# Masked attention stages: the penalties' matmul ahead of the maxima, scores accumulated on it

## The chip, the cores and the metric

One core of a Trainium2 chip runs the whole program. The time is device microseconds of one execution; the median of several runs stands for a kernel. Engines: PE multiplies matrices (PEld loads its stationary operand), ACT exponentiates and copies, DVE reduces and adds, POOL does small vector work, SP issues DMAs. PE writes into PSUM, which has eight banks of 128 x 512 float32.

## The reference, cut to what matters

Four layers of cross and self attention over x (8 x 512 x 256) follow one another; written as six attention stages s, each is

```
q, k, v = heads of x and of its keys        # 16 heads of 16
scores = q @ k^T * 16 ** -0.5                # 512 x 512 for each head
scores = where(mask, -inf, scores)           # stages 0 and 2 (two masks), stage 3 is causal
x = x + softmax(scores) @ v @ Wo             # then an MLP behind stages 0, 2 and 4
```

The last stage has 64 channels a head and is written as a loop of its own ("tail"). Only stages 0 and 2, the masked ones, are touched here; with 8 batches each they are 16 units of attention.

## The kernel before, in words

A softmax needs a maximum for each row. The kernel computes the scores twice: once roughly in bf16 with the queries along the partitions, for DVE to find the maxima (`max_scores`, L678, into the banks psS), and once in float32 with the keys along the partitions (`exp_scores`, L696, into the four banks psT, with the maximum already subtracted through an extra row of Q and K), for ACT to exponentiate (L991). In the masked stages two of the four heads of a step (j = 0, 1) get their mask as a penalty of -2^100, which a matmul of the identity with a bf16 tile of penalties adds in PSUM (L702); the other two (j = 2, 3) are limited after the exponential by DVE (`limit`, L1180). So a masked step exponentiates the pair 2, 3 first and the pair 0, 1 second.

The loop goes over bodies. A body handles three batches at once: the end of the one before (`prev`: output projection, in stages 0, 2 and 4 the MLP), the attention of the current one (`cur`), and the preparation and part of the maxima of the next (`nxt`). It has 16 steps i, for 4 groups of heads times 4 tiles of keys (kt). In each step PE does, in the order of the program, which is the order in which it executes:

- the maxima listed as `before` for this step (two 32-row matmuls, one for each bank of psS; each waits until DVE has read that bank),
- `exp_scores(i)`: it waits for both exponentials of step i - 1, which read the same four banks; then the scores in float32 (32 rows each, four side by side in the array, eight recorded matmuls), then the penalties (two full 128 x 128 bf16 matmuls),
- fills (transposes L645, projections L650 and L657, maxima as rows L762; one shared bank, `small`),
- the maxima listed as `beside`, the matmuls of the probabilities with V (`outputs(i - 1)`, L721, which wait for the exponentials and for DVE's limit), more fills, the maxima listed as `after`.

In which step which maxima and fills stand is written out by hand (`maxima_plan`, `NXT_USES`, `CUR_USES` and the like). In bodies with an MLP inside (14 of the 16 masked ones) one pair of maxima stands `before` in steps 1 to 8 and 13 to 15, a pair `beside` in steps 13 to 15, and step 12 has one beside and one after; the MLP (L779, L788) stands between steps 9 and 10 and uses psT too. The two other masked bodies have one before and one or two further pairs in each step.

Of the kernel before, what the change touches and what calls it, by code (L numbers as in the profile page):

```python
# [6 lines left out]
P = 128  # L7
B = 8
S = 512
D = 256  # L10
C = D // P
T = S // P
# [27 lines left out]
MASKED = (0, 2)  # L40
CAUSAL = 3
# [241 lines left out]
def positive(n):  # L283

    return not isinstance(n, int) or n > 0


def build(nc, x, ctx, ctxT, maskB, maskBT, maskS, maskST, vecs, wa, wm1, wm2, w5, eye, tri, triT, out):
    with ExitStack() as stack:
        def sb(name, shape, dt=F32):  # L290
            return stack.enter_context(nc.sbuf_tensor(name, shape, dt))
# [4 lines left out]
        def semaphore(name):  # L296
            return stack.enter_context(nc.semaphore(name))

        sem = {n: semaphore(n) for n in PER[0]}
# [33 lines left out]
        def count(name, u, k):  # L333

            return u.b * PER[u.s][name] + (AHEAD.get(name, 0) + B * sum(PER[i][name] for i in range(u.s)) + k)
# [72 lines left out]
        pens = sb("pens_sb", [P, 3, T * S], BF16)  # L408
# [12 lines left out]
        identb = sb("identb", [P, P], BF16)  # L421
        onesb = sb("onesb", [P, P], BF16)
        onesf = sb("onesf", [P, DL])
        trib = sb("trib", [P, 2, P], BF16)
# [11 lines left out]
        pensE = [pens[:, 2, :], out5[:, 1, 6 * S:8 * S].bitcast(BF16)]  # L436
# [34 lines left out]
        def masking(tiles, u):  # L471

            return tiles[u.parity if u.s == 0 else 0]

        def rows_of(j):
            return slice(32 * j, 32 * (j + 1))
# [5 lines left out]
        psT = [psT_all[:, i, :] for i in range(4)]  # L482
# [159 lines left out]
        def _(pe):  # L642
# [18 lines left out]
            def max_scores(place, u, i, k, ahead):  # L661

                g, qt = divmod(i, T)
                c, a, q = g // 2, g % 2, u.parity
                n = (qt + 1) * P if u.s == CAUSAL else S
                if qt == 0 and k == 0 and a == 0:

                    if ahead:
                        wait_taken(pe, place, "nxt", place.last("nxt", f"k{c}"))
                    else:  # L670
                        pe.wait_ge(small_read, place.start() + 1)
                    pe.wait_ge(sem["q_low"], count("q_low", u, c + 1))

                for e in range(2):
                    j = 2 * (1 - k) + e
                    if positive(r := count(f"s_read{e}", u, 2 * i + k)):
                        pe.wait_ge(sem[f"s_read{e}"], r)
                    nc.tensor.matmul(psS[e][:, 0:n], Qb[rows_of(j), q, a, c, qt * P:(qt + 1) * P], Kb[rows_of(j), q, c, 0:n],  # L678
                                     start=True, stop=True).then_inc(sem[f"s_full{e}"], 1)

            def exp_scores(place, u, i):

                g, kt = divmod(i, T)
                c, a, q = g // 2, g % 2, u.parity
                q0 = kt * P if u.s == CAUSAL else 0
                if kt == 0:

                    pe.wait_ge(small_read, place.fills("cur", f"m{g}") + 2 if g else place.start() + 1)
                if u.s == 0 and i == 0:
                    pe.wait_ge(sem["pens"], count("pens", u, 2))  # L690

                if positive(k := count("exp_done", u, 2 * i)):
                    pe.wait_ge(sem["exp_done"], k)
                for j in (2, 3, 0, 1) if u.s in MASKED else range(4):
                    plain = u.s != CAUSAL and not (u.s in MASKED and j < 2)
                    last = nc.tensor.matmul(psT[j][:, q0:S], Kf[rows_of(j), q, a, c, kt * P:(kt + 1) * P], Qf[rows_of(j), q, a, c, q0:S],  # L696
                                            start=True, stop=plain)
                    if plain and j % 2:
                        last.then_inc(sem["st_full"], 1)
                for j in range(2 if u.s in MASKED else 4 if u.s == CAUSAL else 0):  # L700
                    if u.s in MASKED:
                        last = nc.tensor.matmul(psT[j], identb[:], masking(pensE, u)[:, kt * S:(kt + 1) * S], start=False, stop=True)  # L702
                    else:
                        last = nc.tensor.matmul(psT[j][:, q0:q0 + P], identb[:], trib[:, 1, :], start=False, stop=True)
                    if j % 2:
                        last.then_inc(sem["st_full"], 1)

            def outputs(place, u, i):

                g, kt = divmod(i, T)  # L710
                q0 = kt * P if u.s == CAUSAL else 0
                if i in (2, 3):
                    wait_taken(pe, place, "cur", f"v{i}")
                pe.wait_ge(sem["exp_done"], count("exp_done", u, 2 * i + 2))
                if u.s in MASKED:
                    pe.wait_ge(sem["limited"], count("limited", u, i + 1))

                if kt == 0 and positive(k := count("o_out", u, g)):
                    pe.wait_ge(sem["o_out"], k)
                for j in range(4):  # L720
                    last = nc.tensor.matmul(psO[32 * j:32 * j + 32, q0:S], V[:, u.parity, kt, head(g, j), :],  # L721
                                            probs[:, i % 2, j, q0:S], start=kt == 0, stop=kt == T - 1)
                last.then_inc(sem["pv_done"], 1)
# [71 lines left out]
            def mlp(place, u, cur, nxt):  # L795

                def maximum_next(n):
                    if nxt is not None:
                        max_scores(place, nxt, n // 2, n % 2, True)

                if cur is not None:
                    pe.wait_ge(sem["exp_done"], count("exp_done", cur, 2 * (MLP_AFTER + 1)))
                for m in range(FC):
                    hidden(place, u, m)
                    maximum_next(m)
                    if cur is None and m >= FC - T - 1:
                        tail_max_scores(m - (FC - T - 1))
                if cur is not None:
                    outputs(place, cur, MLP_AFTER)
                for t in range(T):  # L810
                    for part in range(2):
                        from_hidden(place, u, t, part)
                        maximum_next(FC + 2 * t + part)

            def body(place, prev, cur, nxt):
                units = (cur, nxt)

                def maxima(pairs):
                    for ahead, n in pairs:
                        max_scores(place, units[ahead], n // 2, n % 2, ahead)  # L820

                for i, (before, beside, after) in enumerate(place.body.maxima()):
                    late = place.body.at(2 * i + 1)
                    long = any(use in ("q0", "q1", "k0", "k1", "w") for _, use in late)
                    after_mlp = place.body.mlp and i == MLP_AFTER + 1
                    maxima(before)
                    if cur is None and nxt is None and i in TAIL_TURNS:
                        for name in TAIL_TURNS[i]:
                            tail_fill(name)
                    if cur is not None:  # L830
                        if after_mlp:
                            pe.wait_ge(sem["z_read"], count("z_read", prev, 1))
                        exp_scores(place, cur, i)
                    for owner, use in place.body.at(2 * i):
                        fill(place, owner, use, prev, cur, nxt)
                    if not long:
                        maxima(beside)
                    of = prev if i == 0 else None if after_mlp else cur
                    limited = of is not None and of.s in MASKED and not (place.body.at(2 * i) and late)
                    if of is not None and not limited:  # L840
                        outputs(place, of, (i - 1) % STEPS)
                    if long:
                        maxima(beside)
                    for owner, use in late:
                        fill(place, owner, use, prev, cur, nxt)
                    if limited:
                        outputs(place, of, (i - 1) % STEPS)
                    maxima(after)
                    if place.body.mlp and i == MLP_AFTER:
                        mlp(place, prev, cur, nxt)  # L850
# [112 lines left out]
            for at in range(T * PAIRS):  # L963
                n, kt = divmod(at, T)
# [633 lines left out]
```

## Time and profile before

| | |
|---|---|
| median of 3 runs | 5038.94 us (5037.19 to 5039.55) |
| the profiled execution | 5035.45 us, span 5033.6 us |
| PE busy | 4666.1 us (93%), 24484 matmuls |
| DVE busy | 3036.8 us (60%) |
| ACT busy | 2308.4 us (46%) |
| POOL busy | 1068.9 us (21%) |
| mean granted clock of PE | 0.976 |

A busy share is a mean over stages. Masked bodies take some 107 to 112 us each; the two masked stages lie at 70 to 931 us and 1544 to 2399 us of the span. In a timeline a row is a run of the same instruction of one line; matmuls overlap and their ends are modelled, so the start of the next row tells more than the end of one.

### The profile page before, as it was taken

The numbers are of one execution on the slowest core, as the hardware profiler recorded it, in microseconds if no ns is written. First come the engines' busy times: TensorE is split into PE (matmuls) and PEld (weight loads), VectorE is DVE, ScalarE is ACT, GpSimd is POOL, SyncE is SP. The second block draws the span as 40 slices with busy tenths as digits, with TensorE's granted clock in tenths as the row PEclk, the third lists the DMA queues.
The fourth block names the chain that finished last, engine by engine and source line by source line (L and its number), as shares of the span: only waits on it lengthen the run. The fifth ranks groups of instructions, "written<-read, shape, count | busy, mean of one in ns | idle before, by whom it ended". The sixth has DMA issues, their size and how long they took to land.

```text
span 5033.6 us, 66240 instructions
## 1 busy us (share of the span) xinstructions
PE 4666.1 (93%) x24484; PEld 1880.0 (37%) x24484; DVE 3036.8 (60%) x7970; ACT 2308.4 (46%) x3011; POOL 1068.9 (21%) x991
## 2 busy tenths in 40 slices
PE   6999999989998999999988889999989999999999
PEld 2333333433332333343444433333333333333333
DVE  6777776556767777665565565555534455545554
ACT  4454554456664444434445454444443333333332
POOL 0111211111111211111111111211113333333333
PEclk9999999999999999999999999999999999999999
DMA  1111111121121111001211121111120000000000
GB/s 60 35 51 52 48 41 44 35 87 56 58 66 51 37 37 33 30 31 42 73 61 56 57 71 42 52 37 35 39 77 21 13 1 13 13 13 13 1 13 9
DMA packets 164465, 201.67 MB, mean 40 GB/s; under 512 B 36273, under 2 KB 119601, under 8 KB 162866
## 3 DMA queue, kind: packets, MB, share of 16 engines
q1 hardware_dynamic: 141106, 176.34, 10.5%
q0 software_dynamic: 23040, 21.10, 1.7%
q8 instruction: 197, 3.23, 0.3%
q14 instruction: 122, 1.00, 0.1%
HBM read 128.86 MB, written 68.42 MB: 39 GB/s over the span
## 4 chain that ended last, share of the span: by engine, by line
PE 61%; issue 19%; DVE 14%; ACT 4%; POOL 1%; DMA 1%; DVEq 0%; SPq 0%; POOLq 0%; ACTq 0%
PE psO L721 8%; PE small L650 8%; PE psT L696 6%; PE small L657 5%; PE psT L926 5%; PE psS L678 4%; PE psT L779 3%; DVE nmb L1171 3%; PE psT L650 2%; PE psT L886 2%; PE psO L941 2%; PE psT L896 2%; PE psT L941 2%; PE psT L702 2%; DVE xn L1148 2%
## 5 line engine op out<-in xcount | busy, mean ns | idle before, releaser
L991 ACT ACTIVATE probs<-psT 128x1024 f32<-128x1024 f32 (+3 forms) x1280 | 1159.7, 960 | 1211.2 <-PE psT L696 1042.0
L1171 DVE TENSOR_REDUCE nmb<-psS 128x1 bf16<-128x512 f32 x1024 | 649.8, 685 | 293.4 <-PE psS L678 292.8
L1168 DVE CUSTOM_DVE_ANT_0 out<-psS,pens_sb 128x512 f32<-128x512 f32 x1024 | 665.4, 685 | 250.4 <-issue 248.7
L696 PE MATMUL psT<-low 32*128 32x512 f32 (+3 forms) x5120 | 755.0, 608 | 29.4 <-ACT probs L991 26.5
L721 PE MATMUL psO<-probs,V 128*32 128x512 f32 (+3 forms) x5120 | 670.5, 597 | 20.6 <-DVE probs L1180 19.0
L678 PE MATMUL psS<-out 32*128 32x512 bf16 (+3 forms) x2560 | 595.6, 380 | 97.1 <-DVE nmb L1168 46.4
L1354 DVE TENSOR_REDUCE parts<-psS 128x2 bf16<-128x1024 f32 x256 | 314.9, 1230 | 531.4 <-PE psS L913 531.4
L1097 ACT ACTIVATE probs<-psT 128x1024 f32<-128x1024 f32 x256 | 262.0, 1023 | 524.9 <-PE psT L929 524.9
L678 PEld LDWEIGHTS psS<-out 32*128 32x128 bf16 x2560 | 148.6, 91 | 796.9 <-issue 444.0
L779 PE MATMUL psT<-out,W 128*128 128x512 f32 x768 | 382.9, 620 | 0.4
L1021 ACT ACTIVATE low<-small,vec 128x256 f32<-128x256 f32 (+1 forms) x464 | 261.9, 617 | 232.8 <-PE small L650 232.7
L1499 POOL TENSOR_TENSOR oN<-oN,probs 128x1024 f32<-128x1024 f32 x128 | 300.6, 2349 | 316.1 <-ACT probs L1097 315.8
L1435 POOL TENSOR_TENSOR var<-mhalf 128x4 f32<-128x4 f32 x80 | 16.9, 211 | 1583.6 <-ACT low L1021 1583.6
L1180 DVE TENSOR_TENSOR probs<-probs,parts 128x1024 f32<-128x1024 f32 x256 | 321.5, 1256 | 50.0 <-ACT probs L991 49.6
L1168 DVE CUSTOM_DVE_ANT_0 out<-psS,tri_row 128x384 f32<-128x384 f32 (+3 forms) x512 | 230.8, 486 | 152.8 <-issue 152.5
L1447 POOL DMA_DIRECT2D oN<-o_mid x160 | 100.2, 631 | 984.1 <-DMA o_mid<-out 870.7
L696 PEld LDWEIGHTS psT<-low 32*128 32x128 f32 x5120 | 253.4, 190 | 120.6 <-issue 80.9
L926 PE MATMUL psT<-V 64*128 64x512 f32 x1024 | 289.0, 641 | 2.2 <-ACT parts L1087 1.0
L650 PE MATMUL small<-hT,Wqkv 128*128 128x256 f32 (+1 forms) x656 | 241.4, 491 | 25.9 <-DVE low L1204 17.2
L1041 ACT ACTIVATE gel<-psT,vec 128x512 f32<-128x512 f32 x192 | 131.9, 687 | 287.1 <-PE psT L779 287.1
L1499 POOL TENSOR_TENSOR oN<-probs 128x1024 f32<-128x1024 f32 x64 | 150.5, 2351 | 412.4 <-ACT probs L1097 412.4
L1204 DVE TENSOR_TENSOR low<-low,small 128x512 f32<-128x512 f32 x160 | 109.6, 685 | 176.0 <-PE small L762 176.0
(178 smaller groups left out, 5942.4 us busy)
## 6 DMA issues: line engine op xcount, KB each, us to landing
o_mid<-out SPq DMA_DIRECT2D x160, 256.0 KB, 2.0
oN<-o_mid POOLq DMA_DIRECT2D x160, 128.0 KB, 3.5
oN<-r_mid SPq DMA_DIRECT2D x80, 256.0 KB
x_mid<-xe SPq DMA_DIRECT2D x40, 512.0 KB, 2.9
xw<-x_mid SPq DMA_DIRECT2D x36, 512.0 KB, 4.1
xe<-x_mid SPq DMA_DIRECT2D x36, 512.0 KB, 5.0
cT<-ctxT SPq DMA_DIRECT2D x20, 512.0 KB, 5.5
W<-wm SPq DMA_DIRECT2D x6, 1024.0 KB, 8.5
```

Of the source, the lines that this page charges most:

```text
L650: last = nc.tensor.matmul(dst[:, tokens], w[:, c, cols], src[:, c, tokens], start=c == 0, stop=c == C - 1)
L678: nc.tensor.matmul(psS[e][:, 0:n], Qb[rows_of(j), q, a, c, qt * P:(qt + 1) * P], Kb[rows_of(j), q, c, 0:n], start=True, stop=True).then_in ...
L696: last = nc.tensor.matmul(psT[j][:, q0:S], Kf[rows_of(j), q, a, c, kt * P:(kt + 1) * P], Qf[rows_of(j), q, a, c, q0:S], start=True, stop=p ...
L721: last = nc.tensor.matmul(psO[32 * j:32 * j + 32, q0:S], V[:, u.parity, kt, head(g, j), :], probs[:, i % 2, j, q0:S], start=kt == 0, stop= ...
L779: last = nc.tensor.matmul(psT[m % 2], W1[:, c, m * P:(m + 1) * P], hM[:, c, :], start=c == 0, stop=c == C - 1)
L926: nc.tensor.matmul(psT[j], K5[n % 3][rows, kt * P:(kt + 1) * P], Q5[n % 3][rows, :], start=True, stop=False)
L991: nc.scalar.activation(probs[:, i % 2, two, q0:S], psT_all[:, two, q0:S], ACT.Exp, scale=float(DH) ** -0.5)\
L1168: nc.vector.tensor_tensor_reduce(junk[:, e, 0:n], psS[e][:, 0:n], penalty, 1.0, -3.0e38, ALU.add, ALU.max, at).then_inc(sem[f"s_read{e}"], 1)
L1171: nc.vector.tensor_reduce(at, psS[e][:, 0:n], AX, ALU.max).then_inc(sem[f"s_read{e}"], 1)
L1180: nc.vector.tensor_tensor(two, two, both, ALU.min).then_inc(sem["limited"], 1)
L1354: nc.vector.tensor_reduce(nmb[n % 2][:, qt, 0:P:DL], psS_both[:], AX, ALU.max, negate=True).then_inc(tail_s_read, 1)
L1499: nc.gpsimd.tensor_tensor(pacc[n % 2], before, P5[kt], ALU.add).then_inc(tail_summed, 1)
```

## The change

The penalties of j = 0, 1 go ahead of everything in a masked step: a new function `penalties` waits for the exponentials of the step before (and, in the first one, for the penalties' tile), then opens the two banks with the identity matmuls (`start=True, stop=False`). Then come the maxima `before`, then the scores, which for j = 0, 1 accumulate on what the bank holds (`start=False`) and close it. The wait for the exponentials thus stands ahead of the maxima in the masked stages; in the others nothing changes. Behind the MLP the wait for its last read of psT moves ahead with the penalties. Number and sizes of all matmuls stay, and the second signal to ACT comes from the scores of j = 1.

```diff
+            def penalties(u, i):
+
+                if positive(k := count("exp_done", u, 2 * i)):
+                    pe.wait_ge(sem["exp_done"], k)
+                if u.s == 0 and i == 0:
+                    pe.wait_ge(sem["pens"], count("pens", u, 2))
+                for j in range(2):
+                    nc.tensor.matmul(psT[j], identb[:], masking(pensE, u)[:, i % T * S:(i % T + 1) * S], start=True, stop=False)
+
             def exp_scores(place, u, i):
...
-                if u.s == 0 and i == 0:
-                    pe.wait_ge(sem["pens"], count("pens", u, 2))
-
-                if positive(k := count("exp_done", u, 2 * i)):
+                if u.s not in MASKED and positive(k := count("exp_done", u, 2 * i)):
                     pe.wait_ge(sem["exp_done"], k)
                 for j in (2, 3, 0, 1) if u.s in MASKED else range(4):
-                    plain = u.s != CAUSAL and not (u.s in MASKED and j < 2)
+                    plain = u.s != CAUSAL
                     last = nc.tensor.matmul(psT[j][:, q0:S], Kf[rows_of(j), q, a, c, kt * P:(kt + 1) * P], Qf[rows_of(j), q, a, c, q0:S],
-                                            start=True, stop=plain)
+                                            start=not (u.s in MASKED and j < 2), stop=plain)
                     if plain and j % 2:
                         last.then_inc(sem["st_full"], 1)
-                for j in range(2 if u.s in MASKED else 4 if u.s == CAUSAL else 0):
-                    if u.s in MASKED:
-                        last = nc.tensor.matmul(psT[j], identb[:], masking(pensE, u)[:, kt * S:(kt + 1) * S], start=False, stop=True)
-                    else:
-                        last = nc.tensor.matmul(psT[j][:, q0:q0 + P], identb[:], trib[:, 1, :], start=False, stop=True)
+                for j in range(4 if u.s == CAUSAL else 0):
+                    last = nc.tensor.matmul(psT[j][:, q0:q0 + P], identb[:], trib[:, 1, :], start=False, stop=True)
                     if j % 2:
                         last.then_inc(sem["st_full"], 1)
...
+                    if cur is not None and cur.s in MASKED:
+                        if after_mlp:
+                            pe.wait_ge(sem["z_read"], count("z_read", prev, 1))
+                        penalties(cur, i)
                     maxima(before)
...
                     if cur is not None:
-                        if after_mlp:
+                        if after_mlp and cur.s not in MASKED:
                             pe.wait_ge(sem["z_read"], count("z_read", prev, 1))
                         exp_scores(place, cur, i)
```

## Rows read from the trace of the kernel before

**Rows 1.** Page, part 5: busy us, mean ns, idle us before, what ended it.

```profile
L991 ACT ACTIVATE probs<-psT 128x1024 f32<-128x1024 f32 (+3 forms) x1280 | 1159.7, 960 | 1211.2 <-PE psT L696 1042.0
```

**Rows 2.** Busy time by stretch: two neighbouring bodies, then both masked stages.

```profile
core 0: us, PE busy (x) PEld busy (x) DVE busy (x) ACT busy (x) POOL busy (x), PEclk, DMA share, GB/s
387.00:498.30 111.30, 105.99 (x540) 43.74 (x540) 78.77 (x265) 55.46 (x63) 20.20 (x23) 0.95 0.14 44
498.30:605.50 107.20, 101.78 (x544) 42.37 (x540) 78.94 (x263) 55.43 (x63) 20.07 (x23) 1.00 0.15 46
...
69.90:930.70 860.80, 804.58 (x4164) 326.93 (x4166) 623.87 (x2010) 429.26 (x496) 145.58 (x167) 0.97 0.14 42
...
1543.90:2399.00 855.10, 795.65 (x4130) 322.07 (x4130) 600.21 (x2019) 386.43 (x462) 138.59 (x162) 0.98 0.12 39
```

**Rows 3.** Timeline of PE, steps 7 to the MLP of one body: start us, us.

```profile
420.27 1.23 PE L696 MATMUL psT<-low 32*128 32x512 f32 x8
...
423.40 0.39 PE L678 MATMUL psS<-out 32*128 32x512 bf16 x2
423.63 1.14 PE L696 MATMUL psT<-low 32*128 32x512 f32 x8
424.70 0.61 PE L702 MATMUL psT<-out,identb 128*128 128x512 bf16 x2
425.14 1.88 PE L650 MATMUL small<-cT,Wqkv 128*128 128x512 f32 x4
...
427.95 1.14 PE L696 MATMUL psT<-low 32*128 32x512 f32 x8
...
431.49 0.59 PE L779 MATMUL psT<-out,W 128*128 128x512 f32 x1
```

**Rows 4.** Timeline of ACT, the same stretch.

```profile
421.55 1.94 ACT L991 ACTIVATE probs<-psT 128x1024 f32<-128x1024 f32 x2 [0.41 <-PE psT L696]
...
429.36 1.96 ACT L991 ACTIVATE probs<-psT 128x1024 f32<-128x1024 f32 x2
```

**Rows 5.** Timeline of PE, step 15 of a body and step 0 of the next.

```profile
602.11 1.23 PE L696 MATMUL psT<-low 32*128 32x512 f32 x8
603.27 0.60 PE L702 MATMUL psT<-pens_sb,identb 128*128 128x512 bf16 x2
603.81 0.64 PE L678 MATMUL psS<-out 32*128 32x512 bf16 x2
...
605.47 1.14 PE L696 MATMUL psT<-low 32*128 32x512 f32 x8
...
606.99 0.39 PE L762 MATMUL small<-identb,nmb 128*128 128x128 bf16 x4
```

**Rows 6.** Timeline of PE, step 14: the second maxima and the fill behind.

```profile
599.47 0.63 PE L678 MATMUL psS<-out 32*128 32x512 bf16 x2
600.03 1.13 PE L657 MATMUL small<-Wqkv,cT 128*128 128x256 f32 x4
```

**Rows 7.** Timeline of DVE, the same step: it reads the maxima's scores.

```profile
598.35 0.69 DVE L1168 CUSTOM_DVE_ANT_0 out<-psS,pens_sb 128x512 f32<-128x512 f32 x1
...
598.97 0.68 DVE L1168 CUSTOM_DVE_ANT_0 out<-psS,pens_sb 128x512 f32<-128x512 f32 x1
...
599.90 0.69 DVE L1168 CUSTOM_DVE_ANT_0 out<-psS,pens_sb 128x512 f32<-128x512 f32 x1 [0.24 <-issue]
```

**Rows 8.** Timeline of PE: idle time in brackets, and who ended it (steps 2, 3, 5, 10).

```profile
397.13 1.07 PE L721 MATMUL psO<-probs,V 128*32 128x512 f32 x8 [0.64 <-DVE probs L1180]
...
401.54 0.66 PE L645 MATMUL small<-ident,xn 128*128 128x128 f32 x4 [1.48 <-DVE xn L1148]
...
412.33 1.97 PE L657 MATMUL small<-Wo,oN 128*128 128x256 f32 x8 [0.25 <-ACT low L1021]
...
909.01 0.38 PE L762 MATMUL small<-identb,nmb 128*128 128x128 bf16 x4 [0.67 <-DVE xe L1243]
```

**Rows 9.** Busy time by stretch, columns as in rows 2: around a fall of the clock.

```profile
399.29:402.70 3.41, 1.43 (x10) 0.53 (x6) 3.41 (x7) 2.68 (x4) 1.40 (x2) 1.00 0.13 41
402.70:406.10 3.40, 3.33 (x18) 1.37 (x22) 2.29 (x6) 0.63 (x2) 0.00 (x0) 0.50 0.43 127
```

## The prediction, made before the change was run

> **What bounds the kernel now.** I read the page first, its costliest groups: ACT, the one engine that exponentiates, idles 1211.2 us before its exponentials, 1042.0 of it for PE's scores [rows 1]. In a masked body PE is busy 101.78 of 107.20 us [rows 2]. So ACT waits for PE in the mean, and removing PE time would pay. But the change removes no instruction; it moves the penalties' 512 matmuls (two a step, 16 steps, 16 masked batches, by the code). What counts is which wait ends last at each place. So I went on to the stretches of one masked body (107.20 and 111.30 us, two neighbours [rows 2]), then to the order of time on PE, ACT and DVE in it. I call the maxima ahead of the scores M, the scores S, the penalties P, output matmuls O, fills F, the second maxima of a step M2; numbers of steps are those of the loop over i.
>
> **The loop through ACT.** In steps 7 to 8, S starts at 420.27, the exponentials run from 421.55 to 423.49, and the next S starts at 423.63 [rows 3, 4]. So from S to the first exponential 1.28 us, both exponentials 1.94, and 0.14 from their end to the next S: 3.36 us, and step 8 is one such period after step 7: PE had come to M at 423.40 [rows 3], M ran in the wait's shadow, and S waited. The same 3.36 stands between steps 15 and 0: S 602.11, S 605.47 [rows 5]. Elsewhere PE's own work is longer than the loop, or DVE is the limit.
>
> **Part 1: P and its wait ahead of M and S.** P costs 0.44 us before a fill (424.70 to 425.14 [rows 3]). Before a 32-row matmul it costs 0.54 (603.27 to 603.81 [rows 5]), since PE drains when the tiling of its array changes; I take 0.54 for P ahead of M. Before, P lay behind S and beside the exponentials; it was outside the loop. After, the order is: exponentials end, P, S, exponentials. The loop becomes 3.36 + 0.54 = 3.90 us. P waits for both exponentials at its start, and behind it in PE's order are M, S and all that follows; M no longer covers the wait, and DVE, which reads M, gets it later. ACT gains nothing from the second pair being ready earlier: its second exponential follows the first at once already (both in one 1.94 stretch [rows 4]).
>
> **Part 2: what that costs, step by step** (bodies with the MLP of the previous batch inside; 14 of the 16 masked batches, 7 in each masked stage).
> - Step 7 to 8: P of step 7 would start where M and S did, 420.27; P of step 8 at 420.27 + 3.90 = 424.17, less 0.1, because step 7's P stands behind a full-array fill and needs no drain: 424.07. Then P 0.54 and M with S 1.16 (602.11 to 603.27 [rows 5]): the fill starts at 425.77, not 425.14. **+0.63**, with no idle time of PE named behind it up to 431.49 [rows 3].
> - Step 9: S moves 0.54 later. Its exponentials end at 431.32 [rows 4], and the MLP's first matmul, which takes the same banks, starts at 431.49 [rows 3]. They began at 429.36, 1.41 after S at 427.95, where 1.28 would do, so 0.13 of the 0.54 is taken up by ACT's own work before them: **+0.4**.
> - Step 14: M2 must wait until DVE has read M. M is read at 598.35 and 598.97, M2 is issued at 599.47 behind P, read at 599.90 [rows 6, 7]. M itself stood at 599.47 - 0.54 - 1.16 - 0.02 = 597.75. After, it comes 0.54 later, at 598.29, its reads start at 598.72 (0.43 after M, as 599.47 to 599.90) and end at 599.96; M2's second half may issue only some 0.14 after that, and what is behind it 0.31 later: 600.41 for the fill that now starts at 600.03. **+0.38**. P behind S no longer fills the time in which DVE reads M.
> - Step 15 to 0: the loop gives 602.11 + 3.90 = 606.01 for P of step 0, then P 0.54 and S without M 1.07 (423.63 to 424.70 [rows 3]): fill at 607.62, now at 606.99 [rows 5]. **+0.63**.
> - Steps 6 and 12 (and 7 in the second masked stage): P between O and M, then a fill, has one drain more than S, P, fill: +0.1 each, **+0.2 to 0.3**. Steps 4 and 11: behind a full-array fill one drain goes and one comes: 0.
> - Steps 1 to 3: the loop is again too long for steps 1 and 2 (0.25 to 0.55 us late). But PE waits 0.64 there for DVE's limits, then 1.48 for the normalised tokens [rows 8]. These waits cover it: 0. With that cover gone it would be +0.8.
> - Step 5: the fill behind P waits 0.25 for ACT's copies in one stage and longer in the other: 0; uncovered +0.3. Step 10: the fill behind P waits 0.67 for DVE's residual sum, and only M's 0.3 and a drain are added ahead of it: 0 [rows 8]. Step 13: M waits for DVE's reads, P slips into that wait, but DVE's order decides when M2 goes: 0, at best -0.44.
> The sum for a body is 0.63 + 0.4 + 0.38 + 0.63 + 0.25 = 2.29 us; times 14 it is 32.1. The two masked bodies without an MLP are bound by DVE's maxima for half their steps: I put 0.5 each, between -3 (P in all waits of M) and +5 (0.3 for each step): **+33 us in all**. The profiled execution took 5035.45 us around a span of 5033.6; so 5068. The median of the three runs is 5038.94, 3.5 above it: forecast **5071.5**.
>
> **Bounds of the unknown prices.** The drain of P to M is shown (0.10 [rows 3, 5]); none of its neighbours makes it zero. Accumulating scores onto the penalties in place of the reverse is not shown. PE accumulates in both orders, and the nearest row is P's own pair, 0.44 for two (0.22 each) on banks that S had opened [rows 3]; I take 0, between -0.1 and +0.1 a step (25 us either way at most, and half of the steps are covered). The loops' latencies vary by 0.1 (1.28 or 1.17 to ACT): 3 us.
> The skill speaks against the change at one place: the Trainium skill, TensorEngine Tiling (Array Packing), Key Properties, says that changing the tiling mode drains TensorE. The trace agrees at 0.10 us. It gives no price; by rule alone, with the rows' price at all 256 steps, the sum would be 26 us for drains, while the order of the code gives a new drain in some 3 steps of 16.
>
> **The clock.** PE's granted clock is 1.2 GHz, one half, in 402.70 to 406.10, behind a stretch in which PE was busy 1.43 of 3.41 us [rows 9]; elsewhere it is 2.4 GHz. The two neighbouring bodies differ by such stretches, and so they come or go with small shifts: 111.30 us at a mean clock of 0.95 against 107.20 at 1.00, or 4.1 us for 11 us at half clock [rows 2]. The masked stages have 0.97 of 860.80 and 0.98 of 855.10 us [rows 2], so 52 + 34 = 86 us at half clock, which cost some 33. P moves into step 13's waits and S of step 3 later into its idle stretch (less idle); steps 0, 8 and 9 get new waits of 0.4 to 0.5 (more idle). I forecast no change and keep both ends.
>
> **Rivals.**
> 1. *The clock saves it (faster).* P at step 13 and S at step 3 fill the two stretches behind which the clock falls now. If all 86 us went, -33; with P also filling M's waits in the DVE-bound bodies, -3, and the loop costing half, because ACT starts 0.1 earlier and steps 14 and 15 are really DVE's, +16: 5019. With the loops at their full price it decides only if all 86 us go. For it: PE's idle share where the clock fell [rows 9]. Against: the loops of steps 8 and 0 have no slack at all. The Trainium skill, TensorE: Matmul & The Clock Gate, HAM oscillation, says that gaps in PE's work between bursts bring the slow clock back; the trace agrees as to what precedes it. Chance 0.07.
> 2. *The change costs little (same).* DVE's waits cover steps 8, 14 and 15 too, since DVE is busy 78.94 of 107.20 us [rows 2]; then only step 9 and drains, 0.65 x 14 = +9: 5048. Against: the rows of steps 7 and 8 show PE without idle time behind the wait. Chance 0.12.
> 3. *The new waits lower the clock (slower still).* The body becomes 109.5 instead of 107.2, and all fourteen, not seven, come to hold 10 us at half clock: 33 + 7 x 4.1 = +62: 5101. Chance 0.18.
> 4. *Forecast*, 5055 to 5088: 0.55. The remaining 0.08 lies between 1, 2 and it (5030 to 5055).
>
> **How the numbers follow.** The likeliest is 5071.5. The range leaves out the faster rival, half of the remainder and the far side of rival 3: 5044 to 5100. A measurement of this kernel tells 0.2% (10 us) from no change. Faster by more: 0.07; within: 0.12; slower: 0.81.
>
> **What would show it.** After: P right behind exponentials of the step before with idle time on PE ended by ACT at steps 8, 0 and (at the first hidden matmul) 9; S to S in steps 7 to 8 and 15 to 0 of 3.9, not 3.36; idle time of PE before P, some 0.4 to 0.5 us for each; P 0.54 long; P in step 13 inside M's wait. Bodies of 109.5 at full clock. I am wrong if the bodies at full clock stay at 107.2 (then the loop isn't what bound steps 8 and 0), if steps 1 to 3 show new idle time (then +0.8 more), or if the count of half-clock stretches in the masked stages changes by over 30 us.

## The result and the profile after

| | before | after |
|---|---|---|
| median | 5039.55 us (11 runs, 5030.68 to 5047.3) | 5050.11 us (11 runs, 5043.52 to 5068.82) |
| ratio | | 1.0029, 95% interval 1.0018 to 1.0039 |
| profiled execution | 5035.45 us, span 5033.6 us | 5048.23 us, span 5046.4 us |
| mean granted clock of it | 0.976 | 0.981 |
| ACT idle before its exponentials | 1211.2 us | 1265.3 us |

The kernel is slower by 10.6 us by the medians (by the ratio, some 14.6), where 32.5 was forecast. The order of time and the granted clock tell two stories, and both are needed.

**The steps.** PE after, in steps 7 to the MLP of one body (start us, us; answers to [rows 3]; L688 are the penalties, P; L702 the scores, S; L724 the outputs):

```profile
419.37 0.60 PE L688 MATMUL psT<-out,identb 128*128 128x512 bf16 x2
...
419.92 1.23 PE L702 MATMUL psT<-low 32*128 32x512 f32 x8
...
423.19 0.60 PE L688 MATMUL psT<-out,identb 128*128 128x512 bf16 x2 [0.46 <-ACT probs L998]
...
423.73 1.24 PE L702 MATMUL psT<-low 32*128 32x512 f32 x8
424.90 1.99 PE L650 MATMUL small<-cT,Wqkv 128*128 128x512 f32 x4
...
431.52 2.17 PE L782 MATMUL psT<-out,W 128*128 128x512 f32 x4
```

and ACT there (answers to [rows 4]):

```profile
421.20 1.94 ACT L998 ACTIVATE probs<-psT 128x1024 f32<-128x1024 f32 x2 [0.84 <-PE psT L702]
...
429.52 1.94 ACT L998 ACTIVATE probs<-psT 128x1024 f32<-128x1024 f32 x2 [0.18 <-PE psT L702]
```

The exponentials end at 423.14, P of step 8 starts at 423.19, behind 0.46 us in which PE has nothing to do. S to S is 3.81 us, where [rows 3] had 3.36. From the first matmul of step 7 to the fill of step 8 it is 5.53 us (419.37 to 424.90), before 4.87 (420.27 to 425.14).

Steps 13 to 0 (PE, the next body; answers to [rows 5, 6]):

```profile
591.95 0.61 PE L688 MATMUL psT<-pens_sb,identb 128*128 128x512 bf16 x2
...
597.62 0.60 PE L688 MATMUL psT<-pens_sb,identb 128*128 128x512 bf16 x2
598.16 0.39 PE L678 MATMUL psS<-out 32*128 32x512 bf16 x2
598.17 1.23 PE L702 MATMUL psT<-low 32*128 32x512 f32 x8
599.34 0.39 PE L678 MATMUL psS<-out 32*128 32x512 bf16 x1
599.96 0.39 PE L678 MATMUL psS<-out 32*128 32x512 bf16 x1 [0.23 <-DVE nmb L1175]
...
602.34 0.61 PE L688 MATMUL psT<-pens_sb,identb 128*128 128x512 bf16 x2
...
606.16 0.61 PE L688 MATMUL psT<-out,identb 128*128 128x512 bf16 x2
...
607.77 0.40 PE L765 MATMUL small<-identb,nmb 128*128 128x128 bf16 x4
```

P costs 0.54 ahead of the maxima (597.62 to 598.16). The second maxima of step 14 split, and their second half waits 0.23 us for DVE, which the 0.54 us of P behind S used to cover (598.93 to 599.47 before). The waits for DVE in steps 2 and 3 are still there and have shrunk, from 0.64 and 1.48 us: they took in the delay, as forecast (answers to [rows 8]):

```profile
397.59 1.07 PE L724 MATMUL psO<-probs,V 128*32 128x512 f32 x8 [0.39 <-DVE probs L1187]
...
401.99 0.66 PE L645 MATMUL small<-ident,xn 128*128 128x128 f32 x4 [1.41 <-DVE xn L1155]
```

**The clock.** Busy time by stretch (us, busy us of PE, PEld, DVE, ACT, POOL with counts, granted clock, DMA; answers to [rows 2] and, the last two rows, to [rows 9]); the first two rows are neighbouring bodies, the next four cut the span at the same places of the program as 930.7, 1543.9 and 2399 cut the one before:

```profile
387.40:496.80 109.40, 103.33 (x537) 41.87 (x538) 78.41 (x263) 55.76 (x63) 19.95 (x23) 1.00 0.14 45
496.80:606.20 109.40, 103.33 (x537) 41.86 (x538) 78.38 (x263) 55.76 (x63) 19.94 (x23) 1.00 0.14 45
...
0.00:935.80 935.80, 842.58 (x4254) 337.41 (x4254) 656.01 (x2145) 450.58 (x527) 149.56 (x182) 0.99 0.14 46
935.80:1545.20 609.40, 551.22 (x3371) 212.30 (x3369) 400.94 (x793) 363.79 (x469) 94.09 (x126) 0.98 0.19 61
1545.20:2406.60 861.40, 794.25 (x4129) 315.14 (x4130) 601.78 (x2019) 387.56 (x462) 139.06 (x162) 0.99 0.12 39
2406.60:5046.40 2639.80, 2476.27 (x12742) 1003.30 (x12738) 1377.64 (x3015) 1109.66 (x1553) 685.48 (x521) 0.97 0.10 33
...
399.90:403.30 3.40, 1.43 (x16) 0.54 (x12) 3.40 (x7) 3.19 (x4) 1.56 (x3) 1.00 0.15 43
403.30:406.70 3.40, 3.40 (x25) 1.37 (x25) 3.18 (x11) 1.96 (x3) 0.27 (x1) 1.00 0.34 125
```

Before, five of the fourteen bodies with an MLP had no stretch at 1.2 GHz and lasted 107.2 us; the other nine lasted 108.8 to 112.5. After, eleven have none, and ten of these last 109.4 or 109.5 us. The first masked stage, with what stands ahead of it, takes 5.1 us more (935.8 against 930.7) and the second 6.3 (861.4 against 855.1), together 11.4 of the span's 12.8; the rest is -3.8 and +5.2 in stages whose program didn't change, and whose share of slow clock did. Summed over the trace's records of the granted clock, counting those that begin behind a masked stage's first scores, the masked stages had 82 us at 1.2 GHz before and 31 after (in the fourteen bodies with an MLP: 65 and 10).

The other executions say the same. One of the changed kernel ran at a mean clock of 0.976 and took 5068.82 us; the fastest ran at 0.983 and took 5043.52. Of 27 executions of the kernel before that came with the first four experiments, 13 had 0.976, with a median of 5037.72 us. Between these two, at the same clock, the difference is 31 us. That rests on one execution of the changed kernel; a straight line through all eleven (3.1 us for each 0.001 of mean clock) gives 5065 at 0.976, which is 27 us more.

### The profile page after: what moved, and what is told of

It reads as the page before. It is cut to its first block, busy times and chain, and to the rows that moved or that the text cites. A ratio compares the mean times of both kernels' runs of the same rounds, so it can differ in the third digit from the quotient of the medians.

```text
span 5046.4 us, 66182 instructions
## 1 busy us (share of the span) xinstructions
PE 4664.3 (92%) x24484; PEld 1868.1 (37%) x24484; DVE 3036.4 (60%) x7970; ACT 2311.6 (46%) x3011; POOL 1068.2 (21%) x991
## 4 chain that ended last, share of the span: by engine, by line
PE 58%; issue 20%; DVE 14%; ACT 5%; DMA 2%; POOL 1%; DVEq 0%; SPq 0%; POOLq 0%; ACTq 0%
PE small L650 7%; PE psO L724 7%; PE small L657 5%; PE psT L702 5%; PE psT L933 5%; PE psS L678 4%; PE psT L782 3%; DVE nmb L1178 3%; ACT probs L998 3%; PE psT L650 2%; PE psT L893 2%; PE psO L948 2%; PE psT L903 2%; PE psT L948 2%; DVE nmb L1175 2%
## 5 line engine op out<-in xcount | busy, mean ns | idle before, releaser
L998 ACT ACTIVATE probs<-psT 128x1024 f32<-128x1024 f32 (+3 forms) x1280 | 1159.2, 959 | 1265.3 <-PE psT L702 1094.3
L702 PE MATMUL psT<-low 32*128 32x512 f32 (+3 forms) x5120 | 746.8, 602 | 28.3 <-ACT probs L998 25.5
L724 PE MATMUL psO<-probs,V 128*32 128x512 f32 (+3 forms) x5120 | 662.7, 590 | 16.3 <-DVE probs L1187 14.7
L702 PEld LDWEIGHTS psT<-low 32*128 32x128 f32 x5120 | 249.8, 188 | 102.8 <-issue 64.2
```

Source lines behind the costliest of these rows:

```text
L998: nc.scalar.activation(probs[:, i % 2, two, q0:S], psT_all[:, two, q0:S], ACT.Exp, scale=float(DH) ** -0.5)\
```

## The experiments

Ratios are to the kernel before on the same chips, with 95% intervals. "Slow clock" is the time at 1.2 GHz in the masked stages of the profiled execution, counted as above; before: 82 us, changed kernel: 31 us. It is one execution each, and other executions of the same kernel have other mean clocks. Three theories: **loop** (what P costs ahead of S), **length** and **content** (why the clock rose).

**Undoing a part: only the steps that should be free.** A tuple of steps decides where P stands; elsewhere the old order is kept.

```diff
+P_AHEAD = (0, 1, 2, 3, 4, 5, 6, 8, 10, 11, 12, 13)
...
-                    if cur is not None and cur.s in MASKED:
+                    if cur is not None and cur.s in MASKED and i in P_AHEAD:
                         if after_mlp:
                             pe.wait_ge(sem["z_read"], count("z_read", prev, 1))
                         penalties(cur, i)
```

> The new order in all masked steps but 7, 9, 14 and 15; those four keep the penalties (P) behind the scores (S). Loop theory (a P ahead of S delays the exponentials of its own step, and costs only where the next step, or DVE's reads, wait for them: steps 7, 9, 14, 15): bodies at full clock of 107.5 us (107.2 plus three drains of 0.1), against 109.4 of the changed kernel. Rival (every P that is queued behind the wait for exponentials costs its part): about 12/16 of the 2.2 us stay, 108.9. On the clock: if P in step 13's waits and S in step 3's idle stretch are what keeps PE at full clock (content theory), the half-clock time of the masked stages falls from 86 us to about 30 and the kernel beats the one before: 5039 + 4 - 20 = 5023, ratio 0.997. If it was the length of the bodies (length theory), half-clock time goes back towards 86 us and the ratio is 1.001.

Measured: 0.9997 (0.9985 to 1.0008), bodies at full clock of 107.9 us, slow clock 58 us. Twelve of sixteen steps in the new order cost 0.7 us a body, not 1.7: nearer to the loop theory (0.3) than to its rival. The slow clock is between the two theories: no slow stretch begins in steps 12 or 13, but ten begin in step 3, although P stands ahead there as in the changed kernel, where one does. From S(7) to S(8) it is 3.82 us here too (P of step 8 is ahead): the longer period by itself only moves P from behind S(8) to ahead of it, and what costs is P ahead of S(7).

```profile
381.80:489.70 107.90, 101.61 (x533) 41.88 (x536) 78.30 (x263) 55.67 (x63) 19.93 (x23) 1.00 0.15 45
```

**The complement: only the steps that should cost.** `P_AHEAD = (7, 9, 14, 15)`.

> The complement: the new order in steps 7, 9, 14 and 15 alone. Loop theory: bodies at full clock of 107.2 + 0.45 (step 7) + 0.46 (9) + 0.38 (14) + 0.45 (15), some 108.9 to 109.0, and S to S of 3.8 us in steps 7 to 8 and 15 to 0. Rival (every P costs its part): 107.2 + 4/16 of 2.2 = 107.8. On the clock: content theory leaves steps 3 and 13 as they were and so 86 us of half clock in the masked stages, ratio 1.005; length theory lets some of it go, ratio 1.002 to 1.004.

Measured: 1.0034 (1.0021 to 1.0046), a body of 108.7 us at full clock, slow clock 89 us.

```profile
384.50:493.20 108.70, 101.35 (x532) 42.29 (x539) 78.62 (x263) 55.55 (x63) 20.09 (x23) 1.00 0.14 45
```

PE there, steps 7 and 8 (L707 are the scores):

```profile
416.65 1.23 PE L707 MATMUL psT<-low 32*128 32x512 f32 x8
...
420.01 1.14 PE L707 MATMUL psT<-low 32*128 32x512 f32 x8 [0.23 <-ACT probs L1006]
```

Four steps cost 1.5 us a body, twelve 0.7, together the 2.2 us of all sixteen. The expectation had 3.8 us from S to S here, wrongly: with step 8 in the old order the period of S is 3.36 again (416.65 to 420.01 in its timeline), and P ahead of S(7) and P behind S(8) both lie in the path. The second did so before; the added cost is the first, which had run beside the exponentials. This kernel kept the slow clock that the changed one shed.

**Length alone.** The old order, and ten matmuls more in the MLP.

```diff
                 if cur is not None:
                     pe.wait_ge(sem["exp_done"], count("exp_done", cur, 2 * (MLP_AFTER + 1)))
+                if cur is not None and cur.s in MASKED:
+                    for _ in range(10):
+                        nc.tensor.matmul(psT[3], identb[:], masking(pensE, cur)[:, 0:S], start=True, stop=True)
```

> The kernel before, its order untouched, with ten more 128x512 bf16 matmuls into an unused bank at the start of the MLP of each of the 14 masked bodies that have one: 10 x 0.216 = 2.2 us more PE work in a stretch where PE is always busy, so that bodies at full clock last 109.4 us, as in the changed kernel. Length theory: half-clock time in the masked stages falls from 86 us to about 30, and the time is that of the changed kernel: ratio 1.002 to 1.003. Content theory: the stretches behind which the clock falls (steps 3 and 13) are as before, 86 us stay, and the full 30 us show: ratio 1.006.

Measured: 1.0009 (1.0000 to 1.0018), slow clock 41 us.

```profile
392.80:501.90 109.10, 102.60 (x543) 43.55 (x550) 78.87 (x265) 55.44 (x63) 20.10 (x23) 1.00 0.14 45
```

14 x 1.9 = 27 us of added work cost 4.7 us (5042.44 against 5037.72), with the order of the steps untouched. The median of the mean clocks rose from 0.976 to 0.981; at 3.5 us for each 0.001, the slope over the 79 executions of the kernel before that stand beside the experiments, that is an estimated 17 of the 22 us given back. The content theory, which wanted 1.006, cannot be the whole of it. The length theory wanted 1.002 to 1.003 and was too dear as well: the slow clock also fell outside the masked stages, from 158 to 137 us.

**Half of it.** The same with five matmuls.

> As the run before with five added matmuls, 1.08 us a body: bodies at full clock of 108.3 us. Length theory: half-clock time differs from both 86 us and from that of the kernel with ten, ratio anywhere from 1.000 to 1.004. Content theory: 86 us stay, 15 us more, ratio 1.003.

Measured: 1.0008 (0.9997 to 1.0019), slow clock 79 us. The slow clock stayed, as the content theory had it, but the time is below its 1.003. By median, 13 us less added work is no cheaper at all; the length theory had left this open.

**Content at step 13.** `P_AHEAD = (13,)`.

> The kernel before with the new order in step 13 alone. Bodies at full clock stay at 107.2 us (P runs where PE waits for DVE's reads). Length theory (the length of a body alone decides how much half clock there is): no change, ratio 1.000. Content theory (P in the waits of step 13 keeps PE busy enough there): the half-clock stretches that begin in steps 12 and 13, 27 of the 82 us in the masked stages, go, ratio 0.998; those of step 3 stay.

Measured: 0.9995 (0.9985 to 1.0004), slow clock 58 us. In the bodies with an MLP no slow stretch begins in steps 12 or 13 any more (five did before, 34 us in all), but eleven begin in step 3, where eight did (27 us; this expectation and the next have the two sums the wrong way round). So what stands in step 13 does matter for it, and the gain was partly taken back at step 3; as a time it is inconclusive.

**Content at step 3.** The old order, and five matmuls in the idle time ahead of the transposes.

```diff
+                if use == "x0" and cur is not None and cur.s in MASKED:
+                    pe.wait_ge(small_read, place.fills(who, use) + 1)
+                    for _ in range(5):
+                        nc.tensor.matmul(small[:], identb[:], tri_row[:], start=True, stop=True)
                 if kind == "x":
                     pe.wait_ge(sem["normed"], count("normed", u, 1))
```

> The kernel before, its order untouched, with five 128x512 bf16 matmuls (1.08 us) into the fills' bank ahead of the wait for the normalised tokens in step 3 of the masked stages, where PE sits idle for 1.5 us. No body gets longer at full clock (107.2). Length theory: no change, ratio 1.000. Content theory: the half-clock stretches that begin in step 3, some 34 us of the 82, go, and what they cost with them: ratio 0.997 to 0.998.

Measured: 0.9984 (0.9976 to 0.9993), slow clock 38 us, none of it in step 3. PE there, in one body (L734 are the added matmuls, whose results nobody reads):

```profile
506.53 1.24 PE L734 MATMUL small<-tri_row,identb 128*128 128x512 bf16 x5
508.17 0.65 PE L645 MATMUL small<-ident,xn 128*128 128x128 f32 x4 [0.40 <-DVE xn L1152]
```

Work that is of no use makes the kernel faster, and its bodies at full clock still last 107.2 to 107.3 us: content is a cause too.

**Length on top of the change.** The changed kernel with the ten added matmuls.

> The changed kernel with ten added matmuls in the MLP of each of the 14 bodies (1.9 us a body, as the run with ten added to the kernel before showed): bodies at full clock of 111.3 us. Length theory: the gift of the clock was that of a length of 109.1 to 109.4 us and is lost again, so that half-clock time goes back to 60 to 86 us: ratio 1.0029 + 0.0053 + 0.003 = 1.011. Content theory: the changed kernel's steps 3 and 13 keep the clock at any length, half-clock time stays at 31 us: ratio 1.008.

Measured: 1.0092 (1.0078 to 1.0105), slow clock 55 us; of the bodies with an MLP nine have a slow stretch in step 3 and last 112.7 to 113.0 us. The ratio is between the two; the slow clock is not the content theory's 31 us. The same order of steps that kept the clock at 109.4 us a body lost it at 111.4.

```profile
616.30:729.20 112.90, 106.75 (x547) 43.29 (x548) 78.36 (x263) 55.71 (x63) 19.90 (x23) 0.98 0.14 43
1770.80:1882.20 111.40, 104.25 (x539) 42.06 (x540) 77.22 (x251) 49.43 (x58) 17.78 (x21) 1.00 0.11 35
```

**P behind M.** The maxima go ahead of the wait and of the penalties.

```diff
                     if cur is not None and cur.s in MASKED:
                         if after_mlp:
                             pe.wait_ge(sem["z_read"], count("z_read", prev, 1))
-                        penalties(cur, i)
                     maxima(before)
+                    if cur is not None and cur.s in MASKED:
+                        penalties(cur, i)
```

> The changed kernel with the maxima M ahead of the wait and of the penalties in every masked step: M, wait, P, S. P still opens the bank and S accumulates, and the loop through ACT keeps P. Loop theory: steps 7 to 8 and 15 to 0 stay at 3.8 us; step 14 loses its 0.38; but M no longer runs beside S in the array, which costs 0.2 to 0.4 in each PE-bound step with an M ahead (1, 2, 4, 6, 8, 14: some 1.5 us a body): bodies of 110 to 111 us, ratio 1.005 to 1.008 with the clock where it falls. If instead it is the wait ahead of M that costs, and not P in the loop, bodies go back towards 107.2 us.

Measured: 1.0092 (1.0077 to 1.0107), dearer than expected; a body of 109.9 us at full clock, slow clock 85 us. S to S in steps 7 to 8 and 15 to 0 is 3.7 us: there it is P in the loop that costs and not the wait ahead of the maxima. In step 14 it is the late maxima: from its S to the next it is 4.34 us again, as in the kernel before, where the changed kernel has 4.72. M alone in the array takes 0.32 us where beside S it takes 0.1:

```profile
509.31 0.39 PE L678 MATMUL psS<-out 32*128 32x512 bf16 x2
509.63 0.60 PE L688 MATMUL psT<-pens_sb,identb 128*128 128x512 bf16 x2
510.16 1.14 PE L702 MATMUL psT<-low 32*128 32x512 f32 x8
```

**Both contents at once.** `P_AHEAD = (13,)` and the five added matmuls in step 3.

> Both of the last two edits in one: the new order in step 13 alone, and five added matmuls ahead of the wait for the normalised tokens in step 3, in the masked stages. Content theory: with both places filled, no half-clock stretch begins in the bodies with an MLP (some 35 us are left, all in the two bodies without one), every such body lasts 107.2 us, and the time is below that of the kernel with the added matmuls alone: ratio 0.997. If bodies of 107.2 us fall cold at another place instead, the ratio stays at 0.998 to 1.000.

Measured: 0.9963 (0.9949 to 0.9977), slow clock 41 us; four of the fourteen bodies with an MLP still have a stretch of it, two in step 4 and two in step 13, and none begins in step 3. The expectation wanted none anywhere in them.

**The same in all stages.** Still `P_AHEAD = (13,)`, and added matmuls in that place by stage: `{0: 5, 1: 3, 2: 5, 3: 11, 4: 7}`.

> As the run before, with added matmuls ahead of the same wait in the other stages too (3, 11 and 7 of them a body in stages 1, 3 and 4, where PE sits idle for 0.96, 2.7 and 2.0 us). Content theory: of the 150 us at half clock outside the masked stages a good part goes as well, most of it in stage 3 with 6.8 us a body: ratio 0.993 to 0.996. If the stretches behind DVE's normalisation are not what lowers the clock there, the ratio is that of the run before.

Measured: 0.9923 (0.9911 to 0.9935), 5000.3 us; over the whole span 113 us of slow clock in place of 240. The content theory holds in the untouched stages too. This kernel beats the one before and the changed one.

**The order alone, with the clock held up.** The changed kernel with the added matmuls of the last run, and that run's kernel beside it on the same chip.

> The changed kernel (new order in all masked steps) with the same added matmuls as the run before, so that the clock is high in both and only the order of the penalties differs. Loop theory: 14 bodies of 109.4 in place of 107.2 us, 31 us more than that run, ratio to the kernel before 0.9923 + 0.0061 = 0.998; the masked stages have as little half clock as there. If the new order costs nothing and only the clock spoke, the ratio is 0.992.

> The kernel of the run before the last once more, for the comparison on the same chip: ratio 0.992 to 0.993.

Measured: 5023.56 us, 0.9975 (0.9963 to 0.9986), and 4994.23 us, 0.9916 (0.9902 to 0.9931); the profiled executions at 0.988 and 0.989. The difference is 29.3 us. The clocks were not quite equal: the first had 124 us at 1.2 GHz in its whole span, the second 110, and the masked stages 48 and 27, where the expectation wanted the same. At 0.4 us each, some 6 of the 29.3 are the clock. Bodies:

```profile
388.90:498.30 109.40, 103.37 (x534) 42.22 (x541) 78.58 (x263) 55.78 (x63) 19.97 (x23) 1.00 0.14 45
```

for the changed order, and for the old one but for step 13:

```profile
488.70:595.90 107.20, 101.71 (x534) 42.86 (x541) 78.58 (x263) 55.43 (x63) 20.09 (x23) 1.00 0.15 46
```

## Why the prediction was right and where it failed

- **The loop through ACT** was right. Forecast 3.90 us, measured 3.81: P starts 0.05 us after the exponentials end, S had started 0.14 after.
- **Step 7 to 8**: forecast +0.63, measured +0.66 (5.53 against 4.87). **Step 14**: +0.38, measured +0.38 (597.62 to 600.28 for 597.75 to 600.03). **Step 15 to 0**: +0.63, measured +0.53, from before's 602.09 to 606.99 and after's 602.34 to 607.77. **Step 9**: +0.4, measured +0.27 (fill of step 8 to the MLP, 6.62 against 6.35).
- **What was costed at nothing** nearly stayed at nothing: from S of step 0 to S of step 4 it is 17.3 us in both, DVE's waits cover it. The four places above make 1.84 of the 2.2 us; the rest of the body adds some 0.36, where drains were put at 0.25.
- **The body**: 109.5 us at full clock was forecast, 109.4 measured. 14 x 2.2 is 31 us; at equal clock the executions give 27 to 31, the last pair of runs 24 to 29.
- **A sign that missed**: idle time of PE ahead of P was forecast at steps 8 and 0 and ahead of the MLP. It shows at step 8 (0.46 us); at step 0 it is 0.10 (605.00 + 1.06 to 606.16), and the MLP's first matmul has none named, since delayed work of PE stood there instead. The prices came close all the same.
- **The bodies without an MLP**: their DVE-bound steps kept their period; what else differs there lies within the changes of the clock, and no run separates it.
- **The step that failed is the one on the clock**: "I forecast no change and keep both ends". The slow clock of the masked stages fell by 51 us, more than the 30 that the prediction itself named as the sign of being wrong; at some 0.4 us each that is worth 19 us (the prediction's own price, 4.1 for 11). 31 - 19 = 12, as the masked stages show (11.4). A term of about -19 stood in the sum at nothing. The first rival asked for all of the slow clock and a halved loop on top, and had 0.07; what came was most of the clock's gain and the full loop, a case between the forecast and the rivals that the prediction had no term for. The range, 5044 to 5100, still holds the median, but by its width: nothing in the sum foresaw that the clock would pay for most of the loop.
- **Why the slow clock fell**: the kept traces separate two places. The table counts the slow stretches that begin in steps 3 and 12 or 13 of the fourteen bodies with an MLP, from the clock records and the starts of the scores, one execution each.

| kernel | body at full clock, us | step 3 | steps 12, 13 |
|---|---|---|---|
| before | 107.2 | 8 | 5 |
| five added matmuls in the MLP | 108.0 | 8 | 4 |
| order changed in 7, 9, 14, 15 | 108.7 | 6 | 3 |
| ten added matmuls in the MLP | 109.1 | 2 | 3 |
| P ahead in step 13 alone | 107.2 | 11 | 0 |
| P ahead in 0 to 6, 8, 10 to 13 | 107.9 | 10 | 0 |
| changed kernel | 109.4 | 1 | 0 |
| changed, ten added matmuls | 111.4 | 9 | 0 |
| changed, maxima first | 109.9 | 5 | 7 |
| matmuls added in step 3 | 107.2 | 0 | 4 |
| the same, P ahead in step 13 | 107.2 | 0 | 2 |
| matmuls added in all stages, P ahead in step 13 (both runs) | 107.2 | 0, 0 | 0, 1 |
| changed, matmuls added in all stages | 109.4 | 0 | 2 |

- With P ahead in step 13 and nothing added in step 3 none begins in steps 12 and 13, at any of four lengths; with matmuls added in step 3, at most two do, where it is up to four or five with P behind. That half rival 1 had right. In step 3 the same order gave ten at 107.9, one at 109.4 and nine at 111.4 us, and the old order eight at 107.2 and two at 109.1: there it is the length and not S coming later, which rival 1 named. That the length came out at a good value is luck. Why lengths act so, no run here settles. In the changed kernel a stretch with PE busy 1.43 of 3.40 us was followed by full clock, and before one of 1.43 of 3.41 by half clock [rows 9]; so a share in a stretch that I cut doesn't decide it.
- On the pages that were drawn on: the Trainium skill, TensorEngine Tiling (Array Packing), Key Properties, has a drain at a change of mode; the trace agrees at 0.10 us. The Trainium skill, TensorE: Matmul & The Clock Gate, HAM oscillation, has waits in PE's work bring back the slow clock. The traces agree where five matmuls in the wait of step 3 removed its slow stretches; by itself it doesn't give the dependence on the length.

## What to carry to other kernels

An operation that moves from behind a wait's release to the path ahead of it costs its full length wherever the next round waits for this one, even if the engine does the same work in all; look for such places by the period from start to start, and for the covered ones by who ended the idle time. A longer period alone is not the cost: with P of step 7 behind and P of step 8 ahead it was 3.82 us, and the body paid nothing there. Where a program's mean clock is below 1, look at time against granted clock over several executions before crediting or blaming an edit of 0.3%. And an engine's idle time that isn't on the path may still cost: cheap matmuls with no reader in PE's wait for DVE took 0.8% off this kernel, together with the new order in step 13.

## What the runs showed of the hardware

- PE's clock answers to where idle time sits: five matmuls (1.24 us) in an idle time of 1.5 us removed all eight slow stretches that began there. With such matmuls in all stages but the last, 127 us less at 1.2 GHz went with about 39 us less time.
- It answers to the length of the repeated body too: with steps 0 to 5 in the same order, slow stretches in step 3 numbered ten, one and nine at 107.9, 109.4 and 111.4 us.
- Added work can be nearly free by way of the clock: 27 us of matmuls cost 4.7 (0 to 9 by the interval).
- Opening a bank with a full-array matmul and accumulating 32-row matmuls on it costs nothing beyond the drain that a run here shows: M and S take 1.17 us behind P (423.73 to 424.90), and 1.16 before (602.11 to 603.27).
- Two 32-row bf16 matmuls cost some 0.1 us beside the eight recorded float32 ones in the same tiling (1.17 us with them, 606.70 to 607.77 without, 1.07), and 0.32 us by themselves.
